# Attention weights and tokens transposed by DMA, the identity as products, two PSUM banks for outputs, and queries one slot later

## The reference

```python
x = x + 0.5 * ffn(layernorm(x), w_gate, w_up, w_down)
x = x + attn(layernorm(x), Wq, bq, Wk, bk)
x = x + 0.5 * ffn(layernorm(x), w_gate, w_up, w_down)

def fp4_linear(x, w):        # blocks of 16 along the last dimension
    return einsum('bsk,nk->bsn', fp4_quant_dequant(x), fp4_quant_dequant(w))
def ffn(x, wg, wu, wd):      # 256 -> 704 -> 256
    return fp4_linear(silu(fp4_linear(x, wg)) * fp4_linear(x, wu), wd)
def attn(x, Wq, bq, Wk, bk):
    a = softmax((x @ Wq.T + bq) @ (x @ Wk.T + bk).T / sqrt(256))
    a = eye(512) + a
    a = a - mean(a, axis=-1)
    return a @ x
```

## Time and profile before

| | |
|---|---|
| median of 3 runs | 2682.87 us (2678.78 to 2693.15) |
| the profiled execution, its own time | 2676.35 us |
| its span, first to last instruction | 2674.4 us |
| PE busy | 2157.4 us (81%) |
| DVE busy | 2226.8 us (83%) |
| ACT busy | 1544.6 us (58%) |
| POOL busy | 1082.1 us (40%) |
| mean granted PE clock | 0.932 |
| DMA, share of 16 engines | 27.9% (the main queue) |

### The profile page before, as it was taken

One profiled execution on the slowest core, in us unless ns is written; L12 is line 12 of the kernel. 1 busy time (PEld: TensorE's weight loads), 2 busy tenths in 40 slices (PEclk: granted clock), 3 DMA queues, 4 the chain that ended last, 5 costly groups with the idle time before them and its releaser, 6 DMA issues. The chain is left out here.

```text
span 2674.4 us, 46133 instructions
## 1 busy us (share of the span) xinstructions
PE 2157.4 (81%) x13514; PEld 1247.4 (47%) x13514; DVE 2226.8 (83%) x4089; ACT 1544.6 (58%) x3835; POOL 1082.1 (40%) x1206
## 2 busy tenths in 40 slices
PE   1677888888888888888888888888888888888975
PEld 1344544444444444454444445444544444454542
DVE  5458988888988888898888898888888889888875
ACT  2355665665566556566566566655655656655552
POOL 3234443443343443344444334444434434433332
PEclk6799999999999999999999999999999999999997
DMA  1212233232323223232323222332322322223212
GB/s 49 54 38 49 63 68 68 54 71 57 68 65 70 58 62 71 63 62 66 70 55 70 60 68 62 71 67 59 69 59 63 70 66 58 68 58 71 58 44 57
DMA packets 538947, 165.70 MB, mean 62 GB/s; under 512 B 503712, under 2 KB 538400, under 8 KB 538656
## 3 DMA queue, kind: packets, MB, share of 16 engines
q1 hardware_dynamic: 538656, 162.18, 27.9%
HBM read 19.53 MB, written 16.78 MB: 14 GB/s over the span
## 5 line engine op out<-in xcount | busy, mean ns | idle before, releaser
L1082 PE MATMUL gu_ps<-wgu_hi,xT 128*128 128x512 f16 (+1 forms) x3072 | 946.6, 371 | 68.2 <-DMA xT<-f_dq 34.3
L562 POOL TENSOR_TENSOR tile_area<-tile_area,h_rs 128x704 f32<-128x704 f32 x256 | 354.7, 1386 | 977.6 <-DVE h_rs L984 977.6
L1082 PE MATMUL gu_ps<-wgu_lo,xT 128*128 128x512 f16 (+1 forms) x1536 | 571.2, 372 | 0.0
L1082 PEld LDWEIGHTS gu_ps<-wgu_hi,xT 128*128 128x128 f16 x3072 | 308.5, 100 | 396.7 <-issue 81.1
L1181 PE MATMUL out_ps<-wd_hi,hT 128*128 128x256 f16 x1536 | 358.6, 277 | 116.1 <-DVE x_later L852 55.7
L715 ACT ACTIVATE tile_area<-gu_ps,gu_unit 128x704 f32<-128x704 f32 x256 | 216.4, 845 | 352.8 <-PE gu_ps L1082 349.6
L1181 PE MATMUL out_ps<-wd_lo,hT 128*128 128x256 f16 (+1 forms) x1536 | 373.0, 278 | 0.0
L907 DVE SCALAR_TENSOR_TENSOR tile_area<-gu_ps,gu_unit,tile_area 128x704 f32<-128x704 f32 x256 | 233.9, 914 | 152.1 <-PE gu_ps L1082 121.0
L1082 PE MATMUL out_ps<-xs_hi,pT_hi 128*128 128x256 f16 x512 | 153.7, 300 | 153.3 <-DVE x_later L929 149.6
L770 ACT ACTIVATE h_y<-tile_area 128x704 bf16<-128x704 f32 x256 | 200.8, 784 | 89.2 <-POOL tile_area L562 89.1
L953 DVE SCALAR_TENSOR_TENSOR tile_area<-h_y,tile_area 128x704 f32<-128x704 bf16 x256 | 231.3, 904 | 17.3 <-ACT h_y L770 14.8
(11 more groups left out here) (161 smaller groups left out, 4613.0 us busy)
## 6 DMA issues: line engine op xcount, KB each, us to landing
x<-in_L_attn_x SPq DMA_DIRECT2D x32, 512.0 KB, 3.9
out<-x_later SPq DMA_DIRECT2D x32, 512.0 KB, 3.1
hT<-h_dq SPq DMA_TRANSPOSE x256, 3.1
xT<-f_dq SPq DMA_TRANSPOSE x64, 4.3
w_raw<-in_L_ffn_w_down SPq DMA_DIRECT2D x1, 704.0 KB, 7.5
w_raw<-in_L_ffn_w_gate SPq DMA_DIRECT2D x1, 640.0 KB, 4.6
w_raw<-in_L_ffn_w_up SPq DMA_DIRECT2D x1, 640.0 KB, 5.7
expo<-in_L_attn_Wq SPq DMA_DIRECT2D x1, 256.0 KB, 7.5
```

What stands on the lines that cost most here:

```text
L562: g.tensor_tensor(blocks(h_xq[:, n % 2, :], FB), blocks(hid[:, n % 2, :], FB), per_block(h_rs[:, n % 2, 0:FB], FB), ALU.mult).then_inc(xq_ ...
L1082: ins = t_.matmul(dst, x, y, start=(i == 0), stop=(i == len(todo) - 1))
```

## The change

- The tokens' halves `xs_hi` and `xs_lo` are transposed by DMA from SP's queue into `aT`, instead of on PE with a copy on ACT.
- The weights are scaled on POOL (`prob`) and, from the same exponentials, on ACT to a float16 high half; POOL subtracts to get the low half; both halves of 128 rows are transposed by one DMA into `pT`. PE's transposes, ACT's casts from PSUM and DVE's `pT_lo` go.
- The identity isn't added to `prob`: two products per output, of 128 identity columns times 2^14 (`eye_sp`) with the tile's `xs_hi` and `xs_lo`, go to the same sum.
- `out_ps` has two banks, taken in turn; a product group waits for the addition two turns before.
- Both queries of a sequence start in slots 1 and 3 instead of 0 and 2. Every part of them thus comes one slot later, in all engines' lists.

```diff
-A_TURNS = (("q0", "afront", 3), ("q1", "afront", 3), ("ah", "afront", 2))
-B_TURNS = (("p1", "query", 4), ("al", "afront", 2), ("p0", "query", 3))
+A_TURNS = (("q0", "afront", 3), ("q1", "afront", 3))
...
-            if j in (0, 2) and 0 <= it - 1 < SEQS:
+            if j in (1, 3) and 0 <= it - 1 < SEQS:
                 start(s, "query")
...
-            ap = (sc_ps[:, 0, :], sc_ps[:, 1, :], out_ps[:, :])[u % W_BANKS][:, 0:sum(r for _, r in cols)]
+            ap = (sc_ps[:, 0, :], sc_ps[:, 1, :], out_ps[:, 0, :])[u % W_BANKS][:, 0:sum(r for _, r in cols)]
...
+        def out_bank(turn):
+            return out_ps[:, turn % 2, 0:D]
...
+            def turn_tokens(b, h, pair):
+                if h == 0:
+                    sp.wait_ge(xs_hi_done.sem, xs_hi_done.at(b + 1, pair))
+                else:
+                    sp.wait_ge(xs_lo_done.sem, xs_lo_done.at(b + 1, pair))
...
+                xs = xs_hi if h == 0 else xs_lo
+                sp.dma_start_transpose(aT[:, h, :, :, :].rearrange("p t c k -> p (t c) k"),
+                                       xs[:, :, :].rearrange("p t d -> p (t d)")).then_inc(aT_in.sem, 16)
+            def turn_probs(a, i, pair):
+                sp.wait_ge(p_lo_done.sem, p_lo_done.at(2 * a + i + 1, pair))
...
+                sp.dma_start_transpose(pT[:, i, :, :, :].rearrange("p h t k -> p (h t) k"),
+                                       p16[:, i, :, :].rearrange("p h d -> p (h d)")).then_inc(pT_in[i].sem, 16)
...
+                if s.query[3] is not None:
+                    turn_probs(s.query[3], 0, pair)
+                if s.afront[2] is not None:
+                    turn_tokens(s.afront[2], 0, pair)
                 if s.tile[1] is not None:
                     n = s.tile[1]
                     sp.wait_ge(dl_done.sem, dl_done.at(n + 1, pair))
...
                     sp.dma_start_transpose(hT[:, n % 2, :, :], h_dq[:, n % 2, :]).then_inc(hT_in[n % 2].sem, 16)
+                if s.afront[2] is not None:
+                    turn_tokens(s.afront[2], 1, pair)
+                if s.query[3] is not None:
+                    turn_probs(s.query[3], 1, pair)
...
+                    g.tensor_scalar(s_scale[:, :], s_rsum[:, :], SP, 0.0, ALU.mult, ALU.add).then_inc(scale_done.sem, 1)
...
+                    for i in range(2):
+                        g.tensor_scalar(prob[:, i, :], expo[:, i, :], s_scale[:, i:i + 1], s_nmean[:, i:i + 1],
+                                        ALU.mult, ALU.add).then_inc(prob_done.sem, 1)
+                    for i in range(2):
+                        pool.wait_ge(prob_done.sem, prob_done.at(2 * a + i + 1, pair))
+                        pool.wait_ge(p_hi_done.sem, p_hi_done.at(2 * a + i + 1, pair))
+                        if pair is not None or a >= 1:
+                            pool.wait_ge(pT_in[i].sem, pT_in[i].at(16 * a, pair))
+                        g.tensor_tensor(p16[:, i, 1, :], prob[:, i, :], p16[:, i, 0, :], ALU.subtract).then_inc(p_lo_done.sem, 1)
...
-                    a_.activation(aT_lo[:, :, :].rearrange("p c t -> p (c t)"), tr_b16[:, :], ACT.Copy).then_inc(b_free.sem, 1)
...
-                    a_.activation(aT_hi[:, :, :].rearrange("p c t -> p (c t)"), tr_a16[:, :], ACT.Copy).then_inc(a_free.sem, 1)
...
-                    a_.activation(pT_hi[:, 1, :], tr_b[:, :], ACT.Copy, scale=SP).then_inc(p_hi_done.sem, 1)
...
-                    a_.activation(pT_hi[:, 0, :], tr_b[:, :], ACT.Copy, scale=SP).then_inc(p_hi_done.sem, 1)
+                    act.wait_ge(scale_done.sem, scale_done.at(a + 1, pair))
+                    act.wait_ge(nmean_done.sem, nmean_done.at(a + 1, pair))
+                    for i in range(2):
+                        if pair is not None or a >= 1:
+                            act.wait_ge(pT_in[i].sem, pT_in[i].at(16 * a, pair))
+                        a_.activation(p16[:, i, 0, :], expo[:, i, :], ACT.Identity, scale=s_scale[:, i:i + 1],
+                                      bias=s_nmean[:, i:i + 1]).then_inc(p_hi_done.sem, 1)
...
-                    v.scalar_tensor_tensor(out=pT_lo[:, 1, :], in0=tr_b[:, :], scalar=SP, in1=pT_hi[:, 1, :],
-                                           op0=ALU.mult, op1=ALU.subtract).then_inc(b_free.sem, 1)
...
-                    v.tensor_tensor(prob[:, 0, t * P:(t + 1) * P], prob[:, 0, t * P:(t + 1) * P], ident[:, :],
-                                    ALU.add).then_inc(eye_done.sem, 1)
...
+            def attend(a, i, turn):
+                t = 2 * (a % QPS) + i
+                return products(out_bank(turn), [(pT[:, i, 0, k, :], pT[:, i, 1, k, :], xs_hi[:, k, :], xs_lo[:, k, :])
+                                                 for k in range(TILES)],
+                                [(eye_sp[:, :], xs_hi[:, t, :]), (eye_sp[:, :], xs_lo[:, t, :])])
...
-                    pe.wait_ge(a_free.sem, a_free.at(turn_ah[b] + 1, pair))
-                    pe.wait_ge(b_free.sem, b_free.at(turn_al[b] + 1, pair))
+                    pe.wait_ge(aT_in.sem, aT_in.at(32 * (b + 1), pair))
...
-                    attend(0).then_inc(out_full.sem, 1)
-                    pe.wait_ge(eye_done.sem, eye_done.at(2 * a + 2, pair))
...
-                    turn_weights(1).then_inc(b_full.sem, 1)
+                    pe.wait_ge(pT_in[0].sem, pT_in[0].at(16 * (a + 1), pair))
+                    if pair is not None or turn_att0[a] >= 2:
+                        pe.wait_ge(out_added.sem, out_added.at(turn_att0[a] - 1, pair))
+                    attend(a, 0, turn_att0[a]).then_inc(out_full.sem, 1)
```

175 lines of the change are left out of this document (53 added, 122 removed).

## The result

The changed kernel takes 3061.67 us (median of 4 runs, 3061.03 to 3063.18), the kernel before beside it 2682.61 (4 runs, 2678.78 to 2693.15): 1.140 times as long, with a 95% interval of 1.136 to 1.144. That is 379 us more. The profiled execution has a span of 3059.7 us and a mean granted clock of 0.887. The forecast of 2965 had the sign and the largest term, and was 97 us short; its range of 2750 to 3090 holds the time, close to the upper end.

A forecast was written before the change was run, and what follows sets the result against it. No engine alone bounds the kernel; chains closing inside one slot set it. Stretches 0 + 2.2 - 2.0 + 2.4 + 6.8 = 9.4 us a sequence, over thirty sequences 282 us, give 2965 us; range 2750 to 3090.

The forecast's parts named there:

- D(5) to D(6): From DVE's start of `hid` in slot 5 to slot 6: 13.5 us becomes 11.5, as `pT_lo`, identity additions and a wait leave.
- D(0) to D(1): Between `hid` starts of slots 0 and 1: low token transpose waits behind `hT` on SP, 6.8 us more, the largest term.
- The rival in which the token transpose is hidden: Slot 1's wait doesn't form, the stretch from slot 0's `hid` keeps near 9.7 us: 2761 us, chance 0.12.
- D(6) to D(0): From slot 6's `hid` to slot 0's: PE waits for transposed weights, ACT's sums for the last attention addition; 2.4 us more.
- the loss of clock in slot 6: After PE's wait for transposed weights, products run at a lower granted clock; some 1.5 us lost.
- D(6) to D(7): From slot 6's `hid` to slot 7's: weights landing late and the low clock make it 8.9 us.
- D(7) to D(0): From slot 7's `hid` to slot 0's: last attention addition stands before the front's sums and `silu`; 10.8 us.
- D(3) to D(5): From slot 3's `hid` to slot 5's: longer ACT chain, then POOL's subtractions ahead of `f_xn`; 20.0 becomes 22.2 us.
- D(1) to D(3): From slot 1's `hid` to slot 3's: the maximum moves to slot 3, PE isn't late; unchanged at 18.4 us.
- upper estimate of 4.6 us a sequence: Four new POOL subtractions block DVE by the shared port, four times 1.15 us; sum 14.0 a sequence, 3103 us.
- collisions: Transposes landing in 4.3 us instead of 2.4, or slot 6's subtractions holding DVE: up to 6.1 us a sequence, 3148, chance 0.14.
- The faster rival: Small transfers and subtractions cost nearly nothing, at PE's three transpose waits and before `f_xn`: 2635 us, chance 0.08.

The follow-up runs named there:

- e9: Kernel before with only the identity added by two products instead of DVE's additions: 2666.81 us, 0.9932 of before.
- e11: e9 with the waiting `pT_lo` moved behind the reciprocal `h_rs` of its slot on DVE: 2693.56 us, 1.0045 of before.
- e10: Changed kernel with its two output banks made one again: 3094.32 us, 1.1527 of before.
- e1: Changed kernel with the low token transpose put ahead of `hT` in SP's queue: 2852.87 us, 1.0637 of before.
- e5: e1 with POOL making `f_ve` and `f_rstd` between `prob` and the subtractions: 2848.39 us, 1.0624 of before.
- e2: Changed kernel with the queries started in slots 0 and 2 again: 2987.67 us, 1.1133 of before.
- e4: Kernel before with only the queries started in slots 1 and 3: 2860.61 us, 1.0651 of before.
- e7: Changed kernel with low token transpose ahead of `hT`, attention outputs behind the down products, queries in slots 0 and 2: 2791.36 us, 1.0384 of before.
- e8: Changed kernel with low token transpose ahead of `hT`, attention outputs behind down products, `f_ve` and `f_rstd` between `prob` and subtractions: 2752.48 us, 1.0264 of before.

## Why the forecast was right, and where its size failed

**What bounds the kernel.** That no engine alone is the bound fits the runs: in e9 and e11 DVE was relieved, in e10 PE's bank was taken away, and each time less came of it than the wait in the trace. The forecast was right not to book the waits of the earlier trace rows as a gain, beyond the 2.0 us in D(5) to D(6).

**D(0) to D(1), +7.7 (forecast +6.8).** The step is right in place and order, shown by e1. In the sequence shown `hT` was issued at D(0)+7.1, the low tokens at 8.6 (forecast 8.3), and they landed at 11.8 (forecast 10.9): the landing had been priced at 2.4 us by a line through 1408 and 2048 columns, and is 3.1. The projection took 2.7 to 2.8 us at the low clock, as forecast. The rival in which the token transpose is hidden put its price at 204 us; e1 measures 209. The sum itself doesn't quite close: its named terms (6.7, 1.37, 2.4, 2.7, 1.4, 0.69, 0.6) add to 15.9 and not 16.5, and the 0.6 between them stands in no term. The low tokens landed 0.9 later than forecast, and what follows took 5.5 where 5.6 was left.

**D(6) to D(0), +4.1 (forecast +2.4).** The mechanism held; three sizes failed. First, the transposed weights reach PE at D(6)+5.9, not 4.7: issue 0.4 later, landing 3.2. Second, the loss of clock in slot 6 is 1.6 us where it happens, as priced (1.5), but it happens in 15 of the 26 iterations: D(6) to D(7) is 9.85 to 10.35 in those and 8.65 in the others. Third, in every second iteration PE stands 2.1 to 2.8 us ahead of slot 0, put down to "issue". The hardware loop has two iterations a turn, so I take this for its turn. In 11 of these 13 iterations gate and up of slot 0 then take 6.15 us at a granted clock of 0.72, against 4.47 at 1.00 in the other two. D(7) to D(0) is 11.6 to 14.0 there and 10.9 to 11.4 in the rest (forecast 10.8); in the kernel before the same turn cost 0.1 to 0.9. This term was missing.

It also decides what the clock of slot 6 is worth. Without a turn, D(6) to D(0) is 19.6 where slot 6 kept its clock and 20.9 to 21.3 where it lost it. With a turn it is 22.0 to 22.7 in the six iterations that lost it and in five that kept it: there the 1.6 us change nothing.

**D(3) to D(5), +2.1 (forecast +2.2).** As told, but two errors cancel: D(4) comes 0.4 earlier than forecast and D(5) 0.3 later behind it. The two subtractions of slot 4 take 2.31 us together, as priced; those of slot 6 take 2.91. `f_am` waits 2.6 us for `f_xn` in the sequence shown, and not about 4. A reason stands in DVE's timeline beside the subtractions of slot 4: `h_sl` takes 1.20 us and `h_q` 1.83, against 0.30 and 0.89 in the slots without them, so DVE comes 1.8 us later to its wait. e5 shows that the wait is real and that shortening it gives nothing, since D(5) to D(6) takes it back.

**D(5) to D(6), -2.7 (forecast -2.0).** The sign is as told; no run separates the additions from `pT_lo` here, so why it is 0.7 more stays open.

**D(1) to D(3), +1.2 (forecast 0).** This term was missing: I had booked the scores' maximum as moved from slot 2 to slot 3 and asked no more. In the changed kernel's timelines of POOL and DVE, late in slot 1:

```profile
1495.16 2.24 POOL L597 TENSOR_TENSOR tile_area<-tile_area,h_rs 128x704 f32<-128x704 f32 x1 [5.39 <-DVE h_rs L987]
```

```profile
1495.00 1.16 DVE L896 SCALAR_TENSOR_TENSOR f_t<-f_y,f_xq 128x1024 f32<-128x1024 bf16 x1
1496.19 2.28 DVE L907 SCALAR_TENSOR_TENSOR f_q<-f_y,f_t 128x1024 f16<-128x1024 bf16 x1
```

And in those of e2, the same code with the query a slot earlier:

```profile
1545.25 1.39 POOL L597 TENSOR_TENSOR tile_area<-tile_area,h_rs 128x704 f32<-128x704 f32 x1 [5.40 <-DVE h_rs L987]
```

```profile
1545.09 1.16 DVE L870 TENSOR_REDUCE s_nmax<-sc_ps 128x2 f32<-128x1024 f32 x1
...
1546.87 1.22 DVE L896 SCALAR_TENSOR_TENSOR f_t<-f_y,f_xq 128x1024 f32<-128x1024 bf16 x1
1548.12 1.23 DVE L907 SCALAR_TENSOR_TENSOR f_q<-f_y,f_t 128x1024 f16<-128x1024 bf16 x1
```

In e2, as in the kernel before, the maximum (L870, a reduction of scores out of PSUM) stands beside POOL's multiplication, and neither is slowed: 1.16 and 1.39 us. With the maximum gone to the next slot, `f_t` and `f_q` meet the multiplication, which takes 2.24, and `f_q` 2.28 in place of 1.23. e4, with no DMA transpose of tokens or weights and no subtraction in it, has the same 19.6. So this is the shift's alone, and the place of an operation that reads PSUM had been a cover.

The rule of the Trainium skill that the prediction weighed (SBUF — State Buffer, "SBUF: two separate sides"), that VectorE and GpSimd take one port pair as an exclusive lock, agrees with this, and so does its detail that of VectorE's operations without a fast mode only those with two SBUF inputs take it, which the maximum doesn't have. The upper estimate of 4.6 us a sequence that was drawn from it for the subtractions didn't come, though the holds did: DVE is held 1.8 us beside the pair of slot 4 and 1.1 beside that of slot 6 (`h_s` 1.14 us instead of 0.18), but each time it waits behind them anyway, for `f_xn` or for PE. D(3) to D(5) and D(5) to D(6) together are 0.8 below a forecast that took nothing for them.

**The sum.** 1.2 - 0.1 - 0.7 + 1.7 + 0.9 = 3.0 us a sequence more than forecast, 90 of the 97 us. Taken by parts instead of by stretches: the shift alone costs 6.2 (e4), all else with SP's order mended gives back 1.1 (e1), and SP's order costs 7.3. This holds for this order of the parts only: with the transposes in place, taking the shift out again (e2) gives back 2.3 a sequence and not 6.2, and in the mended kernels (e7 and e8) the shift is no loss at all. The forecast gave the shift no sum of its own; its parts in D(3) to D(5) and D(7) to D(0) were in it, the one in D(1) to D(3) was not.

**Range and chances.** The forecast's own range was 2866 to 3057, and 3061.67 lies just above it; it is inside the stated one by what that allowed for collisions. The collision that was priced, token or weight transposes landing in 4.3 us, didn't come in the changed kernel (medians of 3.1 to 3.5 us), but in e7. Of the signs, "D(1) to D(3) unchanged" failed, the others came, with smaller waits than told (PE 7.2 to 9.5 us for "some 9", `f_am` 2.6 for "about 4"). The faster rival was to decide "where the unknown prices together fall by more than 9.4". e1 took away the largest exposed wait and e8 also moved the outputs, and both stayed above the kernel before; no run had transposes that land faster, so what a landing of 0.5 us would give isn't shown.

What stays open: why the clock falls in 15 of 26 iterations behind much the same wait; why PE stands 2.1 to 2.8 us at what I take for the loop's turn; why e7's and e8's slots rank the other way than e4 and the kernel before; whether slots 0 and 2 with another place for the attended output would do better than e8; and two output areas in the kernel before, which has no bank free for them, wasn't tried.

## What to carry to other kernels

An in-order queue charges a new transfer for everything that stands before it: look up what the instruction ahead waits for, since moving it one place was worth 209 us here. Ask of each wait you remove which later link of the same chain the engine meets next in its list; in e9 it came back a few instructions on, in e11 in the next slot and larger. A shift by one slot isn't free even when no work changes: alone it cost the kernel before 178 us, by what then stands ahead of what on ACT and DVE. Its price isn't fixed either: it was 74 us in the changed kernel (e2), and none in the mended one (e7 and e8).

## What the hardware showed

- Transposing transfers from SBUF to SBUF didn't land faster for being smaller: 128x1024 and 128x1408 float16 both take 3.1 us after issue (medians), 128x2048 takes 4.4. Issued close behind the 512 KB load of `x`, 128x1024 took 3.5 us in the changed kernel and 4.3 to 4.8 in e7. SP is held 1.23 to 1.37 us by most of the smaller ones (up to 2.5 by a few).
- PE behind the wait for `pT` in slot 6 (3.04 to 3.52 us) ran at 1.00 in 11 of the 26 iterations and at 0.50 to 0.74 in 15, with the same instructions and much the same wait (3.49 us at 1.00, 3.44 at 0.61); behind 7.36 us it ran at 0.50, and six products of 512 columns took 2.7 us there and 1.5 in the projection that followed.
- POOL's multiplication (1.39 us) beside DVE's reduction out of PSUM (1.16 us) cost neither anything; beside `f_t` and `f_q`, which read two SBUF tiles each, it took 2.24 us and `f_q` 2.28. POOL's subtraction of 128x512 held DVE operations of 0.30 and 0.89 us to 1.20 and 1.83.
- PE stands 2.1 to 2.8 us (1.3 to 2.0 in the kernel before), put down to "issue", ahead of slot 0 in every second iteration (the hardware loop has two a turn). In the kernel before this made D(7) to D(0) 0.1 to 0.9 us longer, in the changed one 0.7 to 3.1.
